# Attention stage of a decoder layer: loads in parts, projections apart, second norm in step 14, tiles by head group

## The reference, cut to what matters

```
q, k, v = x @ Wq + bq, x @ Wk + bk, x @ Wv + bv          # 16 heads of 8
pos_k   = rel_embeddings @ Wk + bk                        # 64 buckets
c2p     = take_along_axis(q . pos_k, bucket(i - j))
p2c     = swapaxes(take_along_axis(k . pos_k, bucket(j - i)))
probs   = softmax((q . k + c2p + p2c) / sqrt(3 * 8))
a       = layernorm1((probs @ v) @ Wo + bo + x, 1e-7) * ln_scale + ln_bias
x       = layernorm2(x + a, 1e-5)
```

## Time and profile before

| what | us |
|---|---|
| median of three timed runs | 2842.94 |
| the profiled execution, its own time | 2838.59 |
| its span, first to last instruction | 2836.9 |
| TensorE, VectorE, ScalarE, GpSimd busy in the span | 2414.7, 2232.0, 2286.8, 711.7 |
| first scores of block 0 / end of the last norm | 85.45 / 949.9 |

### The profile page before, as it was taken

How to read it: one execution, slowest core, us unless ns; L and a number is a source line. 1 busy time by engine, 2 the same in 40 slices (tenths; PEclk the granted TensorE clock), 3 DMA queues, 4 the chain that set the end, 5 groups by cost and what they waited for, 6 DMA issues and landing times. The chain is left out here.

```text
span 2836.9 us, 64292 instructions
## 1 busy us (share of the span) xinstructions
PE 2414.7 (85%) x18180; PEld 1323.1 (47%) x18199; DVE 2232.0 (79%) x6591; ACT 2286.8 (81%) x4255; POOL 711.7 (25%) x565
## 2 busy tenths in 40 slices
PE   2888888888888337746699999999999999999997
PEld 1555555555555226614344444444444444444443
DVE  3788888788888576785488888888888888888887
ACT  1888888888888353317699999999999999999997
POOL 2334534544444101124311111111111111111114
PEclk7899999999999659977799999999999999999999
DMA  2000000000000100000011111211111121111113
GB/s 78 13 22 12 11 17 16 11 13 20 11 11 12 44 0 1 0 30 0 16 45 53 52 45 45 60 45 45 52 52 45 45 60 45 45 53 51 45 45 89
DMA packets 182540, 96.04 MB, mean 34 GB/s; under 512 B 22539, under 2 KB 179291, under 8 KB 182491
## 3 DMA queue, kind: packets, MB, share of 16 engines
q1 hardware_dynamic: 182491, 95.45, 12.0%
HBM read 78.10 MB, written 4.73 MB: 29 GB/s over the span
## 5 line engine op out<-in xcount | busy, mean ns | idle before, releaser
L1955 DVE TENSOR_TENSOR c_Hl<-c_HF,c_Hh 128x512 f16<-128x512 f32 x1028 | 679.6, 688 | 160.9 <-ACT c_Hh L1842 144.7
L1838 ACT ACTIVATE c_HF<-c_H,c_b 128x512 f32<-128x512 f32 x1028 | 711.0, 692 | 64.2 <-PE c_H L1777 44.3
L1842 ACT ACTIVATE c_Hh<-c_H,c_b 128x512 f16<-128x512 f32 x1028 | 706.4, 687 | 0.0
L1893 POOL TENSOR_TENSOR c_EX<-c_euler,c_D 128x16 f32<-128x16 f32 x65 | 188.6, 2902 | 1194.6 <-DVE c_D L1928 1194.6
L1775 PE MATMUL c_H<-c_Ch,SH 128*128 128x512 f16 x1028 | 390.1, 379 | 0.0
L1777 PE MATMUL c_H<-c_Ch,SH 128*128 128x512 f16 x1028 | 390.0, 379 | 0.0
L1776 PE MATMUL c_H<-c_Cl,SH 128*128 128x512 f16 x1028 | 390.0, 379 | 0.0
L1786 PE MATMUL c_Y<-c_Hh,SH 128*128 128x512 f16 x1024 | 388.1, 379 | 0.3 <-DVE c_Hl L1955 0.3
L1788 PE MATMUL c_Y<-c_Hl,SH 128*128 128x512 f16 x1024 | 388.1, 379 | 0.0
L1787 PE MATMUL c_Y<-c_Hh,SH 128*128 128x512 f16 x1024 | 388.1, 379 | 0.0
L692 DVE CUSTOM_DVE_ANT_0 a_T<-a_S,a_POS 128x128 f32<-128x128 f32 x1024 | 234.8, 285 | 48.0 <-PE a_S L436 41.0
(11 more groups left out here) (300 smaller groups left out, 4372.8 us busy)
## 6 DMA issues: line engine op xcount, KB each, us to landing
c_CWB<-c_rows SPq DMA_DIRECT2D x260, 256.0 KB, 4.1
a_QN<-a_QH SPq DMA_DIRECT2D x128, 32.0 KB, 1.9
a_KN<-a_KH SPq DMA_DIRECT2D x128, 32.0 KB, 1.8
out<-d_O SPq DMA_DIRECT2D x16, 256.0 KB, 2.3
a_QN<-a_QL SPq DMA_DIRECT2D x64, 32.0 KB, 1.9
a_KN<-a_KL SPq DMA_DIRECT2D x64, 32.0 KB, 1.8
CUR<-in_ctx SPq DMA_DIRECT2D x1, 1848.0 KB
c_rows<-c_CWR SPq DMA_DIRECT2D x65, 8.0 KB, 1.4
```

Of the source, the lines that this page charges most:

```text
L1838: act.activation(HF[:, k % 4, :], bH[k % 4][:, :], ACT.Gelu_apprx_tanh, bias=b1[:, g % EXPERTS, f:f + 1], scale=1.0 / WSCALE).then_inc(hf_ ...
L1842: act.activation(Hh[:, g % 2, f, :], bH[k % 4][:, :], ACT.Gelu_apprx_tanh, bias=b1[:, g % EXPERTS, f:f + 1], scale=1.0 / WSCALE).then_inc( ...
L1955: dve.tensor_tensor(Hl[:, g % 2, f, :], HF[:, k % 4, :], Hh[:, g % 2, f, :], ALU.subtract)\
```

## The change

Loads: tokens come in three parts, block 0 and block 1 with a semaphore of their own (SP waits for block 0 before it issues the second), the rest last among the late loads. Engines start on the early weights; GpSimd's copy of block 0 waits for block 0 alone; the late loads are waited for before the first block's body. Five fills of GpSimd move from the constants to behind the copy of block 0. Stacks: one semaphore for each head group, waited for by its first tile. Steps: q is projected in step 1 as before, k in step 2, the values one sequence at a time in steps 10 to 13; the high halves are taken in steps 1 and 2 behind the exponentials, the low ones in 2 and 3, the values are read in 14. Tiles start in step 5, one in each of 5 and 6, then two. GpSimd's subtraction starts with unit 7. The second norm goes to step 14, the residual sums wait only for the first norm of the block before, and GpSimd's first root stands in step 3 of its order.

```diff
-NORM_STEPS = (2, 3, 4, 5, 6, 7, 9)
+NORM_STEPS = (2, 3, 4, 5, 6, 7, 14)
+TILE_STEPS = (5, 6, 7, 7, 8, 8, 9, 9, 10, 10, 11, 11, 12, 12, 13, 13)
+V_STEPS = (10, 11, 12, 13)
-CONSTS, TAB, BUILT = 21, 10, 4
+CONSTS, FILLS, TAB, BUILT = 16, 5, 10, 4
-EARLY_MAX = range(6, 14)
+EARLY_MAX = range(7, 14)
...
+def tiles_of(u):
+    return [n for n, step in enumerate(TILE_STEPS) if step == u]
...
-qn_in, kn_in = Count(sem("qn_in"), 16 * 3 * NG), Count(sem("kn_in"), 16 * 3 * NG)
+qn_in, kn_in = ([Count(sem(n + str(g)), 16 * 3) for g in range(NG)] for n in ("qn_in", "kn_in"))
...
 # SP
-for src, dst in loads + late:
+for src, dst in loads:
     sp.dma_start(dst, src).then_inc(loaded, 16)
+for n in range(2):
+    sp.dma_start(X[:, n * NB:(n + 1) * NB, :], tokens[:, n * NB:(n + 1) * NB, :]).then_inc(x_in, 16)
+    if n == 0:
+        sp.wait_ge(x_in, 16)
+for src, dst in late:          # Wo, bo, ln_scale, ln_bias, tokens[:, 2 * NB:B, :]
+    sp.dma_start(dst, src).then_inc(late_in, 16)
...
 # GpSimd
-def residuals(i):
-    hold(pool, spare_pool, link_s.sem, link_s.at(i, 0))
+def residuals(i, first):
+    if not first:
+        hold(pool, spare_pool, link_s.sem, link_s.at(i, -3))
...
-pool.wait_ge(loaded, LOADS)
+pool.wait_ge(x_in, 16)
 copy_block(0, 0)
+pool.wait_ge(xb.sem, 1)
+pool.memset(table[96:128, :, :, :, :], 0.0).then_inc(filled, 1)
+pool.wait_ge(filled, 1)
+pool.memset(QN[96:128, :, :, :], 1.0).then_inc(filled, 1)
+pool.wait_ge(filled, 2)
+pool.memset(KN[96:128, :, :, :], 1.0).then_inc(filled, 1)
+pool.wait_ge(filled, 3)
+pool.memset(V[:, :, :, :], 0.0).then_inc(filled, 1)
+pool.wait_ge(filled, 4)
+pool.memset(V[:, :, :, DH:DH + 1], 1.0).then_inc(filled, 1)
+pool.wait_ge(filled, FILLS)
...
+        if first:
+            pool.wait_ge(x_in, 32)
+            pool.wait_ge(late_in, LATE)
...
-            if u == NORM_STEPS[5] and not first:
-                power(i - 1, 1)
+            if u in (NORM_STEPS[1], NORM_STEPS[5]) and not first:
+                power(i - 1, (NORM_STEPS[1], NORM_STEPS[5]).index(u))
...
 # TensorE
-if n == 0:
-    pe.wait_ge(qn_in.sem, qn_in.at(i, qn_in.per * (1 + nxt)))
-if n == 2 * NG:
-    pe.wait_ge(kn_in.sem, kn_in.at(i, kn_in.per * (1 + nxt)))
+if j == 0:
+    done = (qn_in, kn_in)[kind][g]
+    pe.wait_ge(done.sem, done.at(i, done.per * (1 + nxt)))
...
 pe.wait_ge(built, BUILT)
+pe.wait_ge(filled, FILLS)
...
+pe.wait_ge(late_in, LATE)       # before the first body, VectorE too
...
                     if u == 1 and not last:
-                        project_qk(i, 1)
+                        project_q(i, 1)
                     if u == 2 and not last:
-                        project_v(i, 1)
-                    for n in range(2 * (u - 6), 2 * (u - 6) + 2):
-                        if 0 <= n < TILES and not last:
+                        project_k()
+                    if u in V_STEPS and not last:
+                        project_v(V_STEPS.index(u))
+                    for n in tiles_of(u):
+                        if not last:
...
 # ScalarE, after exponentials(i, u)
-                    if u == 1 and not last:
-                        high_half(i, 1, 0)
-                        high_half(i, 1, 1)
+                    if u in (1, 2) and not last:
+                        high_half(i, 1, u - 1)
...
 # VectorE
+dve.wait_ge(filled, FILLS)      # before the last rows of table
...
-                    if u == 1 and not last:
-                        low_half(i, 1, 0)
-                        low_half(i, 1, 1)
-                    if u == 2 and not last:
+                    if u in (2, 3) and not last:
+                        low_half(i, 1, u - 2)
+                    if u == 14 and not last:
                         values_in(i, 1)
```

More of the change, by code:

```diff
@@ L196, in attention_stage @@
         bM = bank("M")
-        loaded, consts = sem("loaded"), sem("consts")
+        loaded, late_in, x_in, consts, filled = (
+            sem(n) for n in ("loaded", "late_in", "x_in", "consts", "filled"))
         tab_ps, tab, built = sem("tab_ps"), sem("tab"), sem("built")
-        xb, xT_ps, xT_ok, v_ps, vn_ok, v_ok, kd_ok = (
-            Count(sem(n), 1) for n in ("xb", "xT_ps", "xT_ok", "v_ps", "vn_ok", "v_ok", "kd_ok"))
+        xb, xT_ps, xT_ok, vn_ok, v_ok, kd_ok = (
+            Count(sem(n), 1) for n in ("xb", "xT_ps", "xT_ok", "vn_ok", "v_ok", "kd_ok"))
+        v_ps = Count(sem("v_ps"), NB)
         qk_ps, hi_ok, lo_ok = (Count(sem(n), 2) for n in ("qk_ps", "hi_ok", "lo_ok"))
-        qn_in, kn_in = Count(sem("qn_in"), 16 * 3 * NG), Count(sem("kn_in"), 16 * 3 * NG)
+        qn_in, kn_in = ([Count(sem(n + str(g)), 16 * 3) for g in range(NG)] for n in ("qn_in", "kn_in"))
         a_ps, hm_ok = Count(sem("a_ps"), TILES), Count(sem("hm_ok"), TILES)
@@ L237, in attention_stage @@
                   (dr["bv"].rearrange("(a n) -> a n", a=1).to_broadcast([P, H]), bv_all[:, :])]
-        late = [(dr["x"].rearrange("b s h -> s b h"), X[:, 0:B, :]), (dr["Wo"], Wo[:, :]),
+        tokens = dr["x"].rearrange("b s h -> s b h")
+        late = [(dr["Wo"], Wo[:, :]),
                 (dr["bo"].rearrange("(a n) -> a n", a=1).to_broadcast([P, H]), bo_all[:, :]),
                 (dr["ln_scale"].rearrange("(a n) -> a n", a=1).to_broadcast([P, H]), scale_all[:, :]),
-                (dr["ln_bias"].rearrange("(a n) -> a n", a=1).to_broadcast([P, H]), bias_all[:, :])]
-        EARLY, LOADS = 16 * len(loads), 16 * (len(loads) + len(late))
+                (dr["ln_bias"].rearrange("(a n) -> a n", a=1).to_broadcast([P, H]), bias_all[:, :]),
+                (tokens[:, 2 * NB:B, :], X[:, 2 * NB:B, :])]
+        EARLY, LATE = 16 * len(loads), 16 * len(late)
         @block.sync
@@ L293, in spread_keys @@
                     hold(pool, spare_pool, s_ps.sem, s_ps.at(i, UNITS))
-                hold(pool, spare_pool, qn_in.sem, qn_in.at(i, qn_in.per * (1 + nxt)))
-                hold(pool, spare_pool, kn_in.sem, kn_in.at(i, kn_in.per * (1 + nxt)))
+                for done in qn_in + kn_in:
+                    hold(pool, spare_pool, done.sem, done.at(i, done.per * (1 + nxt)))
                 pool.tensor_copy(QS[:, :, :, :], QN[:, :, :, :].rearrange("p g s b -> p g b s"))
@@ L363, in body @@
                         take_max(i, u)
-                    if u == NORM_STEPS[5] and not first:
-                        power(i - 1, 1)
-                residuals(i)
+                    if u in (NORM_STEPS[1], NORM_STEPS[5]) and not first:
+                        power(i - 1, (NORM_STEPS[1], NORM_STEPS[5]).index(u))
+                residuals(i, first)
                 if not last:
@@ L386, in transposes, with project_q, project_k, project_v @@
                 last.then_inc(xT_ps.sem, 1)
-            def project_qk(i, nxt):
+            def project_q(i, nxt):
                 pe.wait_ge(xT_ok.sem, xT_ok.at(i, 1 + nxt))
                 pe.matmul(bG[0][:, :], Wq[:, :], xT[:, ::-1, :], start=True, stop=True).then_inc(qk_ps.sem, 1)
+            def project_k():
                 pe.matmul(bG[1][:, :], Wk[:, :], xT[:, :, :], start=True, stop=True).then_inc(qk_ps.sem, 1)
[L393 to L396, removed]
+            def project_v(b):
+                pe.matmul(bM[:, b * S:(b + 1) * S], xT[:, :, b], Wv[:, :], start=True, stop=True).then_inc(v_ps.sem, 1)
             def bucket_tile(i, nxt, n):
@@ L500, in _ @@
             pe.wait_ge(tab, 5)
-            project_qk(0, 0)
-            project_v(0, 0)
+            project_q(0, 0)
+            project_k()
+            for b in range(NB):
+                project_v(b)
             pe.wait_ge(tab, TAB)
@@ L562, in high_half @@
                 if nxt:
-                    done = (qn_in, kn_in)[n]
-                    act.wait_ge(done.sem, done.at(i, done.per))
+                    for done in (qn_in, kn_in)[n]:
+                        act.wait_ge(done.sem, done.at(i, done.per))
                 act.activation((QH, KH)[n][:, :], bG[n][:, :], ACT.Identity, bias=(bq, bk)[n][:, :])\
@@ L656, in low_half @@
                 if nxt:
-                    done = (qn_in, kn_in)[n]
-                    dve.wait_ge(done.sem, done.at(i, done.per))
+                    for done in (qn_in, kn_in)[n]:
+                        dve.wait_ge(done.sem, done.at(i, done.per))
                 dve.scalar_tensor_tensor((QL, KL)[n][:, :], bG[n][:, :], (bq, bk)[n][:, :], (QH, KH)[n][:, :],
@@ L868, in body @@
                         norm_step(i - 1, NORM_STEPS.index(u))
-                    for k in range(2 * (u - 6), 2 * (u - 6) + 2):
-                        if 0 <= k < TILES and not last:
+                    for k in tiles_of(u):
+                        if not last:
                             split_rows(i, 1, k)
```

21 lines of the change are left out of this document (8 added, 13 removed).

## The result

The changed kernel takes 2913.38 us (median of four runs, 2912.02 to 2914.71) against 2842.01 of the kernel before (four runs). The ratio is 1.0251, with a 95% interval of 1.0233 to 1.0269: 71 us slower, where 30.6 us faster was forecast. It lies outside the range, and close to rival (c), 2900.

What follows compares the result with a forecast made beforehand. Bound by a load-gated opening chain, then blocks as a ring of three engines, none full. Profiled 2838.6 less 20.1 (opening) and 10.5 (fourteen blocks at 0.75) gives 2808.0; timed, 2842.9 - 30.6 = 2812.3 us; own range 2798 to 2828, 8-in-10 2785 to 2837.

Steps and rivals of the forecast that it cites:

- rival (c): Step 14: every instruction of the second norm held beside GpSimd's queue, 6.3 us a block, 2900 us; chance 0.07.
- Opening: Before the first block: chains start at 10.2 instead of 26.14, 14.4 us gained after fills; with stacks by group 20.1.
- operations held by the fills: Opening: VectorE's small operations beside GpSimd's moved fills lose 1.5 us, bounds 0 and 3.
- Stacks by group: Opening: first table product starts after its own group's stacks, so the whole chain of tiles moves 5.7 us earlier.
- Late loads and cover: Opening: remaining tokens land near 28.5 with 3 us of cover before the query stacks; nothing charged, at most 2.
- Projections apart: Block, steps 1 to 7: k projected after step 2's scores, step 8 starts earlier; gain 1.3 us.
- Norm out of step 9: Block, step 9: without the second norm VectorE's split starts earlier, bound by ScalarE; gain 1.2 us, not 1.9.
- Values in steps 10 to 13: Block: TensorE's four value products lengthen these steps by 0.9 us, bounds 0.5 and 1.9; TensorE over 95% busy.
- Step 14: Block: VectorE's values, second norm and scores make the block's end 0.85 us later after step 14.
- c: Step 14: stall of the second norm beside GpSimd's queued work, taken as 0.4 us, bounds 0 and 6.7.
- rival (b): Step 14: GpSimd's copy gets between two norm instructions, c 1.8 to 2.1 us more, 2837.5 us; chance 0.13.

Runs made afterwards that it cites:

- e5: On e1, TensorE waits for all twelve query stacks before the first query tile, and likewise for keys, as before the change; 2882.98 us (one run).
- e10: Changed kernel, the second norm's four instructions in step 14 multiplying by what stands in PSUM bank M instead of the root; 2805.66 us (one run).
- e2: Changed kernel, second norm left in step 14, GpSimd's residual sums again waiting for all seven norm steps; 2812.27 us, ratio 0.9892.
- e3: Changed kernel, second norm writing over R at fixed addresses instead of into the block's part of X; 2918.81 us (one run).
- e7: Changed kernel, second norm in step 16, GpSimd's key spreading waiting for it, residual sums not; 2787.15 us, ratio 0.9812.
- e6: On e1, the four value products back in step 2 behind the key projection, read in step 3; 2824.07 us, ratio 0.9938.
- e1: Changed kernel with the second norm back in step 9; 2809.1 us, ratio 0.9884.

## Why the prediction was wrong

**Opening: right.** Start 9.92 (forecast 10.2), operations held by the fills: 1.37 and 1.22 us instead of 0.23 and 0.16, some 2.2 us instead of my 1.5. The low halves came 13.4 us earlier, at 31.92; I had 14.4. Of the chain's 2.8 us more from the first copy to there, 0.6 lies ahead of the two holds and stays open. Stacks by group 5.55 (5.7, e5). Late loads and cover: no wait for them appears. 19.0 of 20.1.

**Projections apart: right at equal clock.** The first eight steps of a block come in two lengths, by the granted clock at their start. At full clock they take 442.63 - 424.64 = 17.99 us, and 19.26 before: 1.27, and I had 1.3. With a stretch at half clock they take some 18.9, and 377.78 - 358.11 = 19.67 before. On the average of the thirteen blocks it is 18.70 instead of 19.56, so 0.86.

**Norm out of step 9: right.** Steps 8 and 9 together take 387.24 - 382.14 = 5.10 instead of 6.19, so 1.1 of my 1.2.

**Values in steps 10 to 13: right in sign, too dear.** The four steps take 398.03 - 387.24 = 10.79 instead of 10.22: 0.57, not 0.9. TensorE is busy 8.88 of the 9.70 us from 388.3 to 398.0, not over 95%. Together step 14 came 1.5 us earlier (34.60 instead of 36.14 after step 0, averages of the thirteen), as forecast (1.6).

**Step 14: wrong, and this is the step that failed.** I took c = 0.4 us: one of the four instructions longer by 0.4, the other three at their 0.33. Measured: 6.78 us for 1.11, c = 5.7, in each of 14 blocks (in the last, where GpSimd spreads nothing, the norm took 2.26). From step 14 to the next block's step 0 it took 26.57 us instead of 18.47, averages of the thirteen; I had 0.85 more, it was 8.1. Of these, 6.5 lie ahead of the exponentials of unit 15, and are the hold with the work that I had counted. The other 1.6 lie behind them, at half clock: a term that my sum did not have. With c = 0.4 the rest of my sum would have held: e10, where nothing is held, gains 1.2 us a block against my 0.75, and 2805.66 against 2812.3.

Why did I take it? I read two rows as an order of precedence: a VectorE operation goes before GpSimd's next queued one, and a row of VectorE operations is not broken into. The first is true, but it says only that VectorE gets its turn, not that it keeps it. The second was one case, and thinner than I took it: GpSimd's copy came at 1293.33, with the seventh of the eight instructions, so it shows two instructions let through and not eight. The same line of the same trace, one pass later, has the opposite (VectorE and GpSimd, cross attention, kernel before):

```profile
1304.46 3.19 DVE L1607 TENSOR_SCALAR b_KT<-b_VIS 128x512 bf16<-128x512 f32 x8 [0.23 <-issue]
1306.41 0.63 POOL L1541 COPY X<-b_AT 128x512 f32 x1 [2.38 <-ACT b_AT L1589]
```

Eight instructions took 3.19 us here and 2.78 in the earlier trace rows, and GpSimd's copy its plain 0.63: it had got in between. And the earlier trace rows had shown it at the very line: 1.89 us instead of 1.11, one instruction of four held by a GpSimd operation that started inside the group. With one operation to meet there was one hold; in step 14 there were seven in a row. I named this in rival (b) and dismissed it because that operation "had not been queued behind another".

Rival (c), to which the rule of the Trainium skill ("SBUF — State Buffer", "Who interferes with whom") led at its worst, had 6.3 us a block and 2900; 2913.38 was measured. Its mechanism was right. Its hold was 1 us a block too dear (c = 6.7, measured 5.7), and the low clock, which it did not have either, made up for that: that the sum comes so near is in part luck. The chance of 0.07 was not earned: neither bound was better supported than the other, and I took the value near the end that two thin rows favoured. The looser wait of the residual sums I had even booked as a help ("frees it from the moved norm"); e2 shows that the old wait is worth 101 us.

What stays open: why GpSimd gets its turn after each instruction in the norm, while in one of the two rows of eight the last two instructions were let through. e3 excludes the register operations, and the write to X; nothing here tells what else decides it.

## What to carry to other kernels

Before an operation of VectorE with all operands in SBUF is moved, look what GpSimd does at the new place, and count one GpSimd operation for each instruction: four short ones beside a queue of 2 us operations took 6.8 us, and one short one costs a single hold. Then ask which engine idles meanwhile: here TensorE did, and came back at half clock. A semaphore wait that looks superfluous may be what keeps two engines apart; let GpSimd idle where it has cover (e7: 3.3 us of idling, 2787.15 instead of 2913.38). Where a price lies between bounds as far apart as 0 and 6.7 us and is paid in every block, two rows do not choose between them: search the trace for the case that speaks against the cheap end.

## What the runs showed of the hardware

- VectorE's TENSOR_SCALAR from SBUF to SBUF and GpSimd's queue took turns instruction by instruction: medians of 2084 ns for 336 beside key spreadings of 2.1 us, with addresses from a register and fixed alike (e3). GpSimd lost nothing by it: its spreadings took 2.1 us as before.
- TensorE stood idle from 401.88 to 408.16 us; its granted clock fell from 1.00 to 0.50 at 404.0 and rose at 414.3. From the exponentials of unit 15 to the next step 0 the changed kernel took 16.8 to 17.5 us with 6.6 to 7.6 of them at half clock; at full clock this stretch took 14.89 in the kernel before and in e2.
- The same size with one operand from PSUM was not held once in 44 (343 ns, e10).
- A fill, which only writes, holds VectorE as well: 1.37 us for 0.23 on a 128x128 scaling, 1.22 for 0.16 on 96x4. Not every form: subtractions with two inputs in SBUF, between these two and beside a fill (of V, 16.96 to 18.77), took their 0.21 to 0.22 us as without one (changed kernel):

```profile
17.02 0.22 DVE L829 TENSOR_TENSOR a_POS<-a_POS 96x64 f32<-96x64 f32 x1
...
17.57 1.22 DVE L833 TENSOR_SCALAR a_POS<-a_POS 96x4 f32<-96x4 f32 x1
```

- Four value products put between TensorE's other work (steps 10 to 13) and read in step 14 were 1.36 us a block cheaper than in one piece in step 2 and read in step 3 (e6 against e1).
